# A six-layer decoder on one core: convolution by taps, one projection, and diagonal matrices in a state-space scan

## The chip, the cores and the metric

One core of one Trainium2 chip runs the whole program. The metric is the device time of one execution in microseconds (us); a profiled execution also gives a span, from the first to the last instruction.

## The reference, cut to what matters

Eight sequences of 128 tokens of width 128 (fp32) go through six residual stages, each followed by a layer norm. Stages 1, 2 and 5 are attentions with 16 heads of width 8 (the second and third over a context of 77 tokens), stage 3 is a small mixture, stage 6 a mixture of 8 experts. The change is mostly in stage 4:

```python
scores = gelu(xn @ r_w1 + r_b1) @ r_w2 + r_b2       # one score a token
topk 32 tokens of 128 -> small attention; the other 96 tokens, in order -> state space
xi, z  = split(x_ssm @ in_w)                        # 2 x 256 channels
xc     = silu(conv_b + sum_j shift_j(xi) * conv_w[:, j])         # 4 taps
dtp, Bm, Cm = xc @ xproj_w                          # 8 + 16 + 16 columns
delta  = softplus(dtp @ dt_w + dt_b)
h_t    = exp(delta * A) * h_(t-1) + (delta * xc) * Bm            # 16 states a channel
y      = (sum_s h * Cm + xc * Dp) * silu(z)
x + scattered(y @ out_w, attention output)
```

## The kernel before

Each engine has one instruction stream written by hand, in its own block; the streams meet only at semaphores, and each runs strictly in the order in which it is written. PSUM has 8 banks of 512 fp32 columns. Two rings (`aring`, banks 0 to 3, emptied by ScalarE; `dring`, banks 4 to 7, emptied by VectorE) hand products over in the order of two job lists. `keep_busy` issues idle bf16 products where TensorE would otherwise stand still.

**Stage 4 ahead of the scan** (span 157 to 227 us). VectorE normalises the tokens (XH, L1112), TensorE transposes them and forms the router's scores; VectorE ranks all 128 scores against each other (L1124 to L1132, with a product with `before` on GpSimd in the middle, L568), a product with `after` counts positions (L1582), and L1140 makes a permutation matrix `Perm` for each sequence. TensorE applies it (L1589) to give `xpT`, channels by tokens with the 96 state-space tokens ahead of the 32 chosen ones. The convolution is four accumulated products for each half of the channels and of the tokens, with `conv_w` multiplied into the input weights beforehand (`convin`, L556, L1611). The small attention has its queries masked for each group (`qGa`, L574), 32 score products (L1623), a softmax on VectorE (L1150 to L1160) and 32 output products (L1657), all ahead of the scan. `delta` comes out of xc through a folded weight `Wdt` (L1635), B out of products that use xc as weights (L1641), C out of products of their own (L1648) and goes by DRAM to all partitions. ScalarE and VectorE form the softplus (L763 to L769, L1171 to L1188). Four products give z (L1662). `du` = delta * xc is turned by 12 TensorE transposes (L1704).

**The scan** has 32 steps n (16 states times two halves h of the channels, state s = n // 2). For each state ScalarE scales `duT` by the column of B (`scale`, L795, six pieces of 128x256) and makes two decays (L783). For each step TensorE runs `inputs(n)`, six transposes into one of two PSUM buffers (L1682), VectorE the scan instruction (L1198), GpSimd the product with C (L589), and TensorE `accumulate(n-3)`, 768 columns added through the identity into banks 0 to 2 (L1695). `xD` = xc * Dp (GpSimd, L579) starts those banks.

**After the scan** the gated y and the small attention's output go through their output weights (L1723, L1732) and back to their places through `PermT` (L1741), whose transposes are made ahead of the convolution (L1606).

**The attentions** (`attention_tensor`, `attention_scalar`, `attention_vector`) share a pipeline over the 8 sequences. The weighted values of every sequence go to bank 6 (`weigh`, L1377), so `weigh(7)` waits for `normed`, that is until VectorE has read sequence 6 out of that bank. In the endings, `between` puts other work (transposes of the first half of the result) after iteration B = 8.

The lines that carry most of the argument:

```python
def inputs(n):                                   # TensorE, L1675
    for k in range(NK):                          # NK = 6
        ins = nc.tensor.transpose(dBu[n % NDB][:, 128 * k:128 * (k + 1)],
                                  scaled[s % 2][k][:, 128 * h:128 * (h + 1)], ident[:])
```

Of the kernel before, what the change touches and what calls it, by code (L numbers as in the profile page):

```python
# [28 lines left out]
H, HD = 16, 8  # L29
# [11 lines left out]
NH = DIN // 128  # L41
E1, IW = 8, 256
# [62 lines left out]
class Attention:  # L105


    def __init__(self, sem, name, nk, scale, kM, V, Wo, XB, Xout, masked=False):
# [12 lines left out]
        self.recip_ready = sem(f"{name}_recip_ready")  # L121
# [3 lines left out]
        self.stats_ready = sem(f"{name}_stats_ready")  # L125
        self.var_ready = sem(f"{name}_var_ready")
# [17 lines left out]
    def wait_bank(self, pe, what, i, g=0):  # L144

        if what == "flip" and i >= B:
            pe.wait_ge(self.exp_ready, G * B)
            self.wait_flip_read(pe, i - 1)
            return
        place = PLACE[what, i, g] - len(RING_BANKS)  # L150
        if place >= 0:
# [10 lines left out]
            + ["xnT.0", "xnT.1", "router.0", "router.1", "srow.0", "srow.1", "W5T", "xprojT", "Wdt.0", "Wdt.1", "k5.0", "k5.1", "v5.0", "v5.1", "xpT.0", "xpT.1"]  # L162
            + ["qa", "ka", "permT.0", "permT.1"] + [f"conv.{h}.{c}" for h in range(2) for c in range(2)]
            + [f"delta.{h}.{c}" for h in range(2) for c in range(2)] + [f"z.{h}.{c}" for h in range(2) for c in range(2)]
            + ["x4T.0", "x4T.1", "q5.0", "q5.1", "x5T.0"])
DVE_JOBS = (["kv.0", "kv.1", "kv.2", "kv.3", "v1.0", "k1.1", "v1.1", "q2.0", "q2.1"]
            + ["pooled", "logits8", "cexp", "cT", "up.0", "up.1", "scol"]
            + ["cumU", "va", "BT", "C.0", "C.1", "dposA.0", "dposA.1", "dposS.0", "dposS.1", "dl.0", "dl.1", "x5T.1", "logits6"])
# [8 lines left out]
def _build(nc, ctx, a, out):  # L177
# [11 lines left out]
    before = sb("before", [128, 128])  # L189
# [3 lines left out]
    groupmask = sb("groupmask", [128, G])  # L193
# [30 lines left out]
    Wqkvo4 = sb("Wqkvo4", [128, 4, D]); bqk4 = sb("bqk4", [128, 2]); bv4 = sb("bv4", [128, D])  # L224
    posbias = sb("posbias", [128, D])
    inw4 = sb("inw4", [128, 2 * DIN]); convw = sb("convw", [128, DIN, DC]); convb = sb("convb", [128, NH])
    convin = sb("convin", [128, DC, DIN])
    xprojT = sb("xprojT", [DTR, NH, 128])
    Wdt = sb("Wdt", [128, NH, DIN])
    xproj = sb("xproj", [128, NH, DTR + 2 * DS]); dtw = sb("dtw", [DTR, DIN]); dtb = sb("dtb", [128, NH])  # L230
# [67 lines left out]
    def row(ap, p=128):  # L298
# [26 lines left out]
               (bv4[:], row(a["L1_attn_bv"]))]  # L325
# [3 lines left out]
                (convw[:], a["L1_attn_conv_w"].rearrange("(o n) c -> o n c", o=1).to_broadcast([128, DIN, DC])),  # L329
                (convb[:], a["L1_attn_conv_b"].rearrange("(h p) -> p h", p=128)),  # L330
                (xproj[:], a["L1_attn_xproj_w"].rearrange("(h p) n -> p h n", p=128)),
                (dtw[:], a["L1_attn_dt_w"]), (dtb[:], a["L1_attn_dt_b"].rearrange("(h p) -> p h", p=128)),
# [24 lines left out]
    def spare(t):  # L357
# [3 lines left out]
    dA = [big[:, (2 + i) * W768:(3 + i) * W768] for i in range(2)] + [spare(X[0])]  # L361
# [6 lines left out]
    scaled = [[att[:, 1536 + 256 * k:1536 + 256 * (k + 1)] for k in range(NK)],  # L368
              [qTflat[:, 256 * k:256 * (k + 1)] for k in range(4)] + [att[:, 3072 + 256 * k:3072 + 256 * (k + 1)] for k in range(2)]]
    hst = [big[:, (6 + i) * W768:(7 + i) * W768] for i in range(2)] + [spare(sq)]  # L370
    hC = [big[:, (8 + i) * W768:(9 + i) * W768] for i in range(2)] + [spare(XB), spare(ctxN)]
    NDA, NDB, NHS, NHC = len(dA), len(dBu), len(hst), len(hC)
    kM2flat = kM2[:].rearrange("p j b n -> p (j b n)")
    xD = kM2flat[:, 0:2 * W768]
# [3 lines left out]
    sp_abs = big[:, 2 * W768:4 * W768].rearrange("p (h n) -> p h n", h=NH)  # L378
    sp_exp = big[:, 4 * W768:6 * W768].rearrange("p (h n) -> p h n", h=NH)
    sp_log = big[:, 6 * W768:8 * W768].rearrange("p (h n) -> p h n", h=NH)  # L380
    sp_relu = big[:, 8 * W768:10 * W768].rearrange("p (h n) -> p h n", h=NH)
    PADT = DC - 1 + T
    xpT = sb("xpT", [128, B, PADT])
    hrT = big[0:D // 2, 2 * B * T:3 * B * T].rearrange("p (b t) -> p b t", b=B)
    Srow = big[:, 0:B * T].rearrange("p (b t) -> p b t", b=B)
    scol = sb("scol", [128, B]); gt = big[:, B * T:2 * B * T].rearrange("p (b t) -> p b t", b=B); eq = V2full[:, 2 * NH * W768:2 * NH * W768 + B * T].rearrange("p (b t) -> p b t", b=B)
    rank = sb("rank", [128, B]); ties = sb("ties", [128, B]); sel = sb("sel", [128, B]); unsel = sb("unsel", [128, B]); cumU = sb("cumU", [128, B])
    pos = sb("pos", [128, B]); posa = sb("posa", [128, B])
    Perm = gt; PermT = eq
    qTa = ctxT[:].rearrange("p b t -> p (b t)")[:, 0:B * KSEL].rearrange("p (b k) -> p b k", b=B); kMa = att[:, 1536:1536 + J * B * KSEL].rearrange("p (j b k) -> p j b k", j=J, b=B); va = R[:, 0:2, :]  # L390
    Pa = convw[:].rearrange("p n c -> p (n c)").rearrange("p (n k) -> p n k", k=KSEL)
    PaT = XB[:].rearrange("p b d -> p (b d)").rearrange("p (n k) -> p n k", k=KSEL)
    mxa = sb("mxa", [128, 2 * H]); sma = sb("sma", [128, 2 * H])
    oaT = R[:, 4:6, :]
    oa_heads = Pa
    qGa = att[:, 3072:4096].rearrange("p (g b k) -> p g b k", g=G, b=B)
    Crows = att[0:DS, 0:W768]
# [19 lines left out]
    def _(sp):  # L417
# [4 lines left out]
        dring.wait_copied(sp, "C.1")  # L422
# [20 lines left out]
    def _(pool):  # L443
# [13 lines left out]

        P_.memset(ones_col[:], 1.0)
# [6 lines left out]
        P_.memset(before[:], 0.0)  # L465
# [89 lines left out]
        for j in range(DC):  # L555
            ins = P_.tensor_tensor(out=convin[:, j, :], in0=inw4[:, 0:DIN], in1=convw[:, :, j], op=ALU.mult)  # L556
# [40 lines left out]
    def _(act):  # L597
# [124 lines left out]
        for c in range(2):  # L722
            copy_out(f"srow.{c}", half(Srow, c), bank4, bias=rb2[:])
# [1105 lines left out]
```

## Time and profile before

| | us |
|---|---|
| median of 3 runs | 460.2 (457.71 to 460.31) |
| the profiled execution | 459.13 |
| its span | 457.3 |
| mean granted TensorE clock | 0.976 of full speed |

The profile is of one execution. A line number is that of the kernel before. In the chain of waits each piece is what the next one waited for; a fp32 product has two records (x2) for each matmul, a transpose one. Matmul records overlap, so the pitch (time of a run of them in the chain, divided by their count) is the price, not the length of one record.

### The profile page before, as it was taken

The numbers are of one execution on the slowest core, as the hardware profiler recorded it, in microseconds if no ns is written. First come the engines' busy times: TensorE is split into PE (matmuls) and PEld (weight loads), VectorE is DVE, ScalarE is ACT, GpSimd is POOL, SyncE is SP. The second block draws the span as 40 slices with busy tenths as digits, with TensorE's granted clock in tenths as the row PEclk, the third lists the DMA queues.
The fourth block names the chain that finished last, engine by engine and source line by source line (L and its number), as shares of the span: only waits on it lengthen the run. The fifth ranks groups of instructions, "written<-read, shape, count | busy, mean of one in ns | idle before, by whom it ended". The sixth has DMA issues, their size and how long they took to land.

```text
span 457.3 us, 9931 instructions
## 1 busy us (share of the span) xinstructions
PE 404.7 (88%) x3990; PEld 265.1 (58%) x3990; DVE 284.4 (62%) x697; ACT 234.2 (51%) x433; POOL 138.6 (30%) x118
## 2 busy tenths in 40 slices
PE   3788998999989978997689999989999799999992
PEld 2445675546765836662466666754677456666662
DVE  5785985754757554326499888763466554444546
ACT  1225654737567055766699999314455552222220
POOL 5829643300013124130098989310001100000001
PEclk9899999999999988998899999999999999999997
DMA  7320000000000000003013332052000000000001
GB/s 184 78 72 1 3 4 2 1 3 1 4 4 0 1 0 2 1 0 93 16 69 97 112 97 76 1 187 90 3 3 4 2 0 1 0 0 2 0 1 46
DMA packets 17023, 14.42 MB, mean 32 GB/s; under 512 B 6435, under 2 KB 14147, under 8 KB 16979
## 3 DMA queue, kind: packets, MB, share of 16 engines
q1 hardware_dynamic: 15680, 13.09, 9.7%
q10 hardware_dynamic: 1299, 0.71, 0.5%
q8 instruction: 32, 0.52, 0.5%
q14 instruction: 12, 0.10, 0.1%
HBM read 13.22 MB, written 0.57 MB: 30 GB/s over the span
## 4 chain that ended last, share of the span: by engine, by line
PE 69%; DVE 13%; ACT 11%; issue 3%; DMA 1%; POOL 1%; ACTq 0%; POOLq 0%; DVEq 0%
PE PS L1695 7%; PE PS L1756 6%; PE PS L1760 6%; PE PS L1369 6%; PE PS L1787 6%; PE PS L1315 4%; PE PS L1301 4%; PE PS L1348 4%; ACT att L633 3%; PE PS L1682 3%; PE PS L1384 3%; PE PS L1611 2%; ACT att L795 2%; PE PS L1431 2%; PE PS L1310 2%
## 5 line engine op out<-in xcount | busy, mean ns | idle before, releaser
L633 ACT ACTIVATE att<-PS 77x512 f32<-77x512 f32 (+1 forms) x96 | 51.7, 591 | 45.7 <-PE PS L1372 45.7
L904 DVE TENSOR_REDUCE mxp<-PS 128x4 f32<-128x308 f32 (+1 forms) x96 | 48.0, 537 | 31.8 <-PE PS L1348 31.8
L496 POOL TENSOR_TENSOR rstd<-ve,neg_half 128x1 f32<-128x1 f32 x24 | 13.3, 556 | 120.1 <-DVE ve L966 120.1
L830 ACT ACTIVATE kM<-PS 128x512 f32<-128x512 f32 x32 | 19.1, 597 | 56.3 <-PE PS L1756 56.3
L1198 DVE TENSOR_TENSOR_SCAN big<-big,PS 128x768 f32<-128x768 f32 x22 | 38.2, 1746 | 7.2 <-PE PS L1682 7.2
L1254 DVE TENSOR_TENSOR big<-kM,PS 128x512 f32<-128x512 f32 x32 | 21.9, 688 | 27.3 <-PE PS L1760 26.0
L490 POOL TENSOR_TENSOR rstd<-ve,neg_half 128x4 f32<-128x4 f32 x6 | 6.2, 1032 | 103.7 <-DVE ve L860 103.7
L1301 PE MATMUL PS<-negsel,identb 128*128 128x512 bf16 x140 | 33.9, 386 | 2.2 <-DVE big L1006 1.7
L1756 PE MATMUL PS<-xT,V 128*128 128x512 f32 x64 | 32.9, 596 | 0.8 <-DVE xT L1242 0.8
L1760 PE MATMUL PS<-xT,V 128*128 128x512 f32 x64 | 32.7, 592 | 0.0
L1787 PEld LDWEIGHTS PS<-big 128*128 128x128 f32 x256 | 29.7, 192 | 3.3 <-issue 3.3
L1787 PE MATMUL PS<-big 128*128 128x128 f32 x256 | 29.7, 275 | 0.0
L795 ACT ACTIVATE att<-big,BT 128x256 f32<-128x256 f32 x64 | 27.1, 492 | 0.7 <-DVE big L1202 0.7
L527 POOL TENSOR_TENSOR hr<-hvar,half_bh 77x8 f32<-77x8 f32 (+1 forms) x7 | 22.8, 3265 | 9.4 <-DVE hvar L887 9.4
L1301 PEld LDWEIGHTS PS<-negsel,identb 128*128 128x128 bf16 x140 | 13.1, 99 | 20.1 <-issue 4.5
L1372 PE MATMUL PS<-flipped,negsel 32*77 32x128 bf16 (+1 forms) x384 | 24.5, 216 | 0.0
L1695 PE MATMUL PS<-big,ident 128*128 128x512 f32 (+1 forms) x64 | 23.1, 486 | 0.0
L1275 DVE SCALAR_TENSOR_TENSOR R<-PS,aff,R 128x128 f32<-128x128 f32 x56 | 15.8, 345 | 11.2 <-PE PS L1787 11.2
L1369 PE MATMUL PS<-qT,kM 32*77 32x128 f32 x512 | 20.9, 276 | 1.8 <-ACT att L633 1.1
L783 ACT ACTIVATE big<-big,Aneg 128x760 f32<-128x760 f32 x22 | 19.6, 914 | 2.9 <-DVE big L1188 2.9
L1760 PEld LDWEIGHTS PS<-xT,V 128*128 128x128 f32 x64 | 12.2, 190 | 15.3 <-issue 14.8
L1682 PE MATMUL PS<-ident,att 128*128 128x128 f32 x128 | 19.4, 275 | 1.0 <-ACT att L795 1.0
(349 smaller groups left out, 896.7 us busy)
## 6 DMA issues: line engine op xcount, KB each, us to landing
kM<-Cdram SPq DMA_DIRECT2D x6, 384.0 KB, 3.5
XH<-Cdram SPq DMA_DIRECT2D x5, 384.0 KB, 3.4
xT<-Cdram SPq DMA_DIRECT2D x5, 384.0 KB, 3.4
V<-in_L_ffn_Wg SPq DMA_DIRECT2D x1, 1024.0 KB, 5.4
V<-in_L_ffn_Wu SPq DMA_DIRECT2D x1, 1024.0 KB, 8.0
convw<-in_L_attn_conv_w SPq DMA_DIRECT2D x1, 512.0 KB
out_x<-X SPq DMA_DIRECT2D x2, 256.0 KB, 2.3
ctxN<-in_ctx ACTq DMA_DIRECT2D x1, 308.0 KB
```

Of the source, the lines that this page charges most:

```text
L633: A_(PT[0:nk, i % 2, g], bank4(at.bank("exp", i, g), nk), ACT.Exp, scale=at.scale)\
L795: ins = A_(scaled[s % 2][k], duT[:, k, :], ACT.Identity, scale=BT[:, k, s:s + 1])
L904: V_.tensor_reduce(mxp[:, b % 3, g, 0:J], PS[:, at.bank("max", b, g), 0:J * nk].rearrange("p (j k) -> p j k", j=J), axis=AX.X, op=ALU.max) ...
L1198: V_.tensor_tensor_scan(hst[m % NHS], dA[m % NDA], dBu[m % NDB], 0.0, ALU.mult, ALU.add)\
L1301: M_(PS[:, bank, :], identb[:], negsel[:].rearrange("p j t -> p (j t)"), start=True, stop=True)
L1369: M_(PS[0:nk, at.bank("exp", b, g), j * T:(j + 1) * T], at.kM[rows(g), j, b, :], qT[rows(g), b, :], start=not at.masked, stop=False)
L1372: ins = M_(PS[0:nk, at.bank("exp", b, g), j * T:(j + 1) * T], negsel[rows(g), j, 0:nk], upper(flipped)[rows(g), (b - 1) % 2, 0:T], start=F ...
L1682: ins = nc.tensor.transpose(dBu[n % NDB][:, 128 * k:128 * (k + 1)], scaled[s % 2][k][:, 128 * h:128 * (h + 1)], ident[:])
L1695: ins = M_(y_piece(h, lo, hi), ident[:], hC[n % NHC][:, lo:hi], start=False, stop=(n // NH == DS - 1 and (h, lo) != (0, 512)))
L1756: M_(PS[:, n % 2, :], Wg6[:, e, i * 128:(i + 1) * 128], half(xT, c), start=True, stop=True)\
L1760: M_(PS[:, 2 + n % 2, :], Wu6[:, e, i * 128:(i + 1) * 128], half(xT, c), start=True, stop=True)\
L1787: ins = M_(PS[:, 4 + (2 * e + c) % 4, b4 * D:(b4 + 1) * D], hidE[e % 2][:, i, b * T:(b + 1) * T], Wd6[:, NI * e + i, :], start=(i == 0), s ...
```

## The change

1. **Convolution.** `token_in(b)`, eight products of 512 columns ahead of the permutation, gives xi and z of every token in token order (`XI`); `inner_inputs` then permutes xi (16 products of 96 columns). The first tap is a ScalarE activation, the other three taps are 12 multiply-adds on VectorE. `convin` and its products go.
2. **One projection.** `proj(c)` gives dt, B and C in 40 rows with two products a half; `delta_in(c)` uses 41 rows of it, one of them ones, so that the bias comes along. B is transposed out of it (6 small transposes). The softplus loses its Relu on ScalarE and works on halves of the tokens in place of halves of the channels.
3. **Ranking.** The sums over scores become 16 bf16 products with a column of ones; GpSimd is out of the chain.
4. **Small attention.** Values are made in four masked versions (32 products); the scores are taken by 32-row groups without `qGa`; weights are transposed on TensorE; 32 products of 32 columns and 4 of 256 (`weighted_values`) stand within the scan, after inputs(4), with the division by the sums on VectorE between scan instructions.
5. **z** is permuted within the scan: 16 products of 96 columns (`z_in`, after inputs 17, 19, 21, 23), with copies on ScalarE. `PermT` is made after the scan.
6. **Diagonals.** In place of scaling duT (128x256) and transposing, ScalarE makes six diagonal 128x128 matrices of B a state, and TensorE multiplies duT by them. `xc * Dp` becomes a product with a diagonal.
7. **Attention endings.** The last sequence's weighted values go to bank 4, `between` moves one iteration later, the flips of iterations 8 and 9 use banks 7 and 5 and wait for less. K and V of stage 5 are made before the router, partly on VectorE.

```diff
     def bank(self, what, i, g=0):
         if what == "flip" and i >= B:
-            return 7
+            return 5 if i == B + 1 else 7
...
+    def out_bank(self, b):
+        return 4 if b == B - 1 else 6
...
             def weigh(b):
-                if b:
+                if b == B - 1:
+                    at.wait_flip_read(pe, B - 2)
+                elif b:
                     pe.wait_ge(at.normed, b)
...
+        V_.tensor_tensor(lower, Srow, wide(scol[:], [128, B, T]), ALU.is_lt)
+        for b in range(B):
+            V_.scalar_tensor_tensor(equal[:, b, :], Srow[:, b, :], scol[:, b:b + 1], after[:], ALU.is_equal, ALU.mult)\
+                .then_inc(event("compared"), 1)
...
+        def token_in(b):
+            product(aring, f"XI.{b}", xT[:, b, :], inw4[:])
...
+        def inner_inputs(c):
+            pe.wait_ge(event("perm"), c + 1)
+            aring.wait_copied(pe, f"XI.{HB * c + HB - 1}")
+            for h in range(NH):
+                for b4 in range(HB):
+                    ins = M_(PS[:, 4 + NH * c + h, b4 * TS:(b4 + 1) * TS], XI[:, c * HB + b4, 0, 128 * h:128 * h + 128],
+                             Perm[:, c * HB + b4, 0:TS], start=True, stop=True)
...
+                    V_.scalar_tensor_tensor(a_, x_, convw[:, h, j:j + 1], a_, ALU.mult, ALU.add).then_inc(event("conv"), 1)
...
         def inputs(n):
-            pe.wait_ge(event("scaled"), s + 1)
+            if s:
+                pe.wait_ge(event("scaled"), s)
             if n >= NDB:
                 pe.wait_ge(event("h_ready"), n - NDB + 1)
             for k in range(NK):
-                ins = nc.tensor.transpose(dBu[n % NDB][:, 128 * k:128 * (k + 1)],
-                                          scaled[s % 2][k][:, 128 * h:128 * (h + 1)], ident[:])
+                ins = M_(dBu[n % NDB][:, 128 * k:128 * (k + 1)], duT[:, k, 128 * h:128 * (h + 1)], diagB[s % 2][:, k, :],
+                         start=True, stop=True)
...
         for n in range(1, NH * DS):
             inputs(n)
+            if n == 4:
+                weighted_values()
+            if n >= 17 and n % 2 and n < 25:
+                z_in((n - 17) // 2)
             if n >= 3:
                 accumulate(n - 3)
...
         def scale(s):
             for k in range(NK):
-                ins = A_(scaled[s % 2][k], duT[:, k, :], ACT.Identity, scale=BT[:, k, s:s + 1])
+                ins = A_(diagB[s % 2][:, k, :], ident[:], ACT.Identity, scale=BT[:, k, s:s + 1])
```

## Rows read from the trace of the kernel before

**Rows 1.** The page: its span.

```profile
span 457.3 us, 9931 instructions
```

**Rows 2.** The chain of waits before the scan: start us, us, engine, tile, line.

```profile
162.90 1.28 ACT L606
...
177.84 1.24 DVE big L1140
...
179.12 2.06 PE PS L1589 x16
...
189.41 7.95 PE PS L1611 x24
...
198.02 5.43 PE PS L1635 x16
203.44 2.58 PE PS L1641 x24
206.03 4.39 PE PS L1648 x8
```

**Rows 3.** Timeline of choosing the tokens: start, us, engine, line, operation, shapes.

```profile
168.44 0.17 DVE L1122 COPY scol<-PS 128x8 f32<-128x8 f32 x1 [4.60 <-PE PS L1562]
...
169.94 3.27 POOL L568 TENSOR_TENSOR V<-V,before 128x1024 f32<-128x1024 f32 x1 [8.16 <-DVE V L1124]
...
173.15 2.65 POOL L477 MEMSET V<- 77x3072 f32 x1
...
174.77 1.06 DVE L1131 TENSOR_SCALAR unsel<-rank 128x8 f32<-128x8 f32 x1
```

**Rows 4.** Groups by shape, 166 to 224 us: count, busy us, mean ns.

```profile
L1172 DVE TENSOR_TENSOR big<-big 128x768 f32<-128x768 f32 x2 | 1.9, 959 | 0.1
...
L1152 DVE TENSOR_TENSOR convw<-PS,mxa 128x256 f32<-128x256 f32 x4 | 1.4, 417 | 0.0
```

**Rows 5.** Chain of waits: other products with known shapes.

```profile
71.42 1.12 PE PS L1384 x32
...
379.11 3.57 PE PS L1787 x32
```

**Rows 6.** Windows: us, busy of PE, PEld, DVE, ACT, POOL, granted clock.

```profile
215.00:220.00 5.00, 0.00 (x0) 0.00 (x0) 4.86 (x10) 1.42 (x2) 0.00 (x0) 0.99 0.50 182
220.00:223.00 3.00, 2.79 (x13) 2.82 (x14) 0.94 (x2) 1.24 (x2) 0.00 (x0) 0.50 0.02 5
247.00:290.00 43.00, 42.83 (x214) 28.65 (x214) 38.48 (x23) 42.91 (x82) 39.64 (x22) 1.00 0.27 83
```

**Rows 7.** Timeline of the scan's first inputs and last sums.

```profile
226.76 1.50 PE L1682 MATMUL PS<-ident,att 128*128 128x128 f32 x12 [0.97 <-ACT att L795]
...
292.09 1.45 PE L1695 MATMUL PS<-ctxN,ident 128*128 128x256 f32 x4
```

**Rows 8.** The chain of waits within the scan.

```profile
230.65 2.40 ACT att L795 x6
233.05 0.82 ACT big L783
...
249.69 0.66 PE PS L1682 x6
250.34 1.29 PE PS L1695 x4
```

**Rows 9.** Groups by shape within the scan.

```profile
L1198 DVE TENSOR_TENSOR_SCAN big<-big,PS 128x768 f32<-128x768 f32 x22 | 38.2, 1746 | 7.2 <-PE PS L1682 7.2
...
L589 POOL TENSOR_TENSOR big<-big,kM 128x768 f32<-128x768 f32 x6 | 10.9, 1826 | 27.5 <-DVE big L1198 27.4
```

**Rows 10.** Timeline at the ends of the first and third attention.

```profile
70.11 1.08 ACT L633 ACTIVATE att<-PS 128x512 f32<-128x512 f32 x2
...
355.16 1.07 ACT L633 ACTIVATE att<-PS 77x512 f32<-77x512 f32 x2
...
361.73 1.06 PE L1756 MATMUL PS<-xT,V 128*128 128x512 f32 x2
```

More of the change, by code:

```diff
@@ L390, in _build @@
[L390 to L393, printed above, removed]
+    Perm = X[0]; PermT = masks.rearrange("p (b t) -> p b t", b=B)
@@ new lines, in _ @@
+        negated_exp(0)
+        act.wait_ge(event("small_attention"), 1)
+        A_(Pa[:], Pa[:], ACT.Exp, scale=1 / math.sqrt(HD)).then_inc(event("sp_exp"), 1)
+        negated_exp(1)
+        for c in range(2):
+            w = slice(c * W384, (c + 1) * W384)
+            act.wait_ge(event("sp_exp"), 2 * c + 1)
+            A_(sp_log[:, :, w], sp_exp[:, :, w], ACT.Ln, bias=1.0).then_inc(event("sp_log"), 1)
+        for k in range(2):
+            act.wait_ge(event("turned"), k + 2)
+            A_(half(PaT, 1 - k), bank4(1 - k), ACT.Copy).then_inc(event("chosen_copied"), 1)
@@ L812, in _ @@
                 decay(NH * s + 4)
-        A_(zs[:], zs[:], ACT.Silu).then_inc(event("z_ready"), 1)
+            if s == 0:
+                values_copy(1)
+            if 8 <= s < 12:
+                z_copy(s - 8)
+        act.wait_ge(event("z_copied"), 2 * NH)
+        A_(zs[:], zs[:], ACT.Silu).then_inc(event("z_gate"), 1)
+        for c in range(2):
+            act.wait_ge(event("turned"), c + 4)
+            A_(half(PermT, c), bank4(3 + 4 * c), ACT.Copy).then_inc(event("z_copied"), 1)
         for c in range(2):
@@ L1189, in _ @@
-        for h in range(NH):
-            dve.wait_ge(event("delta_ready"), h + 1)
-            V_.tensor_tensor(du[:, h, :], delta[:, h, :], xc[:, h, :], ALU.mult).then_inc(event("du_ready"), 1)
         def scan(m):
@@ L1548, in _, with values @@
             ins.then_inc(dring.full, 1)
-        loaded(pe, "l4")
-        x_transposed("xnT", XH, event("xh4"), 1, idle=15)
+        loaded(pe, "l5")
+        transposes("W5T", [W5[:, k, :] for k in range(4)], 128, 128)
+        aring.wait_copied(pe, "W5T")
+        product(aring, "k5.0", W5T[:, 1, :], half(ctxT, 0), cols=HB * NC)
+        def values(c):
+            row_products(dring, f"v5.{c}", [ctxT[:, b, :] for b in range(c * HB, (c + 1) * HB)], W5T[:, 2, :], NC)
+        values(0)
+        product(dring, "k5.1", W5T[:, 1, :], half(ctxT, 1), cols=HB * NC)
+        loaded(pe, "l4", "ssm")
+        x_transposed("xnT", XH, event("xh4"), 1, idle=2)
         for c in range(2):
@@ L1563, in _ @@
         ins.then_inc(dring.full, 1)
-        loaded(pe, "l5")
-        transposes("W5T", [W5[:, k, :] for k in range(4)], 128, 128)
-        loaded(pe, "ssm")
-        i = fill(aring, "xprojT")
-        for h in range(NH):
-            ins = nc.tensor.transpose(PS[0:DTR, i, h * 128:(h + 1) * 128], xproj[:, h, 0:DTR], ident[:])
-        ins.then_inc(aring.full, 1)
-        aring.wait_copied(pe, "xprojT")
-        for h in range(NH):
-            product(aring, f"Wdt.{h}", xprojT[:, h, :], dtw[:], cols=DIN)
@@ L1576, in _ @@
-        aring.wait_copied(pe, "W5T")
-        for c in range(2):
-            product(aring, f"k5.{c}", W5T[:, 1, :], half(ctxT, c), cols=HB * NC)
+        for b in range(1, 5):
+            token_in(b)
+        i = fill(dring, "rank")
+        for b in range(B):
+            pe.wait_ge(event("compared"), b + 1)
+            M_(PS[:, i, b:b + 1], lower[:, b, :], onesb[:], start=True, stop=False)
+            ins = M_(PS[:, i, b:b + 1], equal[:, b, :], onesb[:], start=False, stop=True)
+        ins.then_inc(dring.full, 1)
```

619 lines of the change are left out of this document (338 added, 281 removed).

## The prediction, made before the change was run

> **What bounds the kernel now.** I read the chain of waits first, because it tells where time can be won at all, then the windows for busy time and clock, then groups by shape for prices. The span is 457.3 us [rows 1]. The change touches four stretches of it.
>
> Ahead of the scan the chain is a relay: TensorE's products, one engine's reading of them, the next products [rows 2]. Its long pieces are the convolution (7.95), the folded delta product (5.43), B (2.58) and C (4.39). Nothing there overlaps well: from 215 to 220 us TensorE does nothing while VectorE ends the softplus, and its granted clock is 0.50, 1.2 GHz, in the next 3 us [rows 6]. The first transposes of the scan start at 226.76 and its last sum ends at 292.09 + 1.45 = 293.54: the scan is 66.8 us [rows 7].
>
> Within the scan three engines are nearly level. A state costs ScalarE 2.40 + 2 x 0.82 = 4.04 us. It costs TensorE two steps of 0.66 (six transposes) and 1.29 (768 columns of sums), 3.90 [rows 8]. VectorE needs 2 x 1.75 = 3.49 and GpSimd 2 x 1.83 = 3.65 [rows 9]. From 247 to 290 us ScalarE is busy 42.91 of 43.00 us and TensorE 42.83, at full clock [rows 6]. So ScalarE leads by only 0.14 us a state: whatever is taken off it is worth little unless TensorE gets cheaper too.
>
> **The change: the scan.** A fp32 product with 128x128 weights and 128 columns costs 3.57 / 16 = 0.223 us (x32 are two records for each of 16 products) [rows 5]. A fp32 transpose of the same size costs 0.66 / 6 = 0.11 [rows 8]. inputs(n) replaces six of these by six of those: 1.34 in place of 0.66. A step is then 1.34 + 1.29 = 2.63 us of TensorE against 2.02 now, +0.61, and 32 steps give **+19.5**. ScalarE gets cheaper: 256 columns take 0.40 and 760 take 0.82 [rows 8], so 0.83 ns a column and 0.29 for 128; a state is 6 x 0.29 + 1.64 = 3.4 us. It is hidden now, as are VectorE and GpSimd. The gain on ScalarE goes nowhere, and TensorE is the only bound, with no slack.
>
> That changes the cost of what is moved into the scan, all of it on TensorE. weighted_values: 32 products with 32-column weights. The nearest row has 16 of them, of 128 columns and in four column groups, in 1.12 us, 0.07 each [rows 5], so 2.0 at most for the 32 with shorter columns, and 0.4 for the four sums of 256 columns: 2.4. Bounds: 1.0 (half the columns' price) and 3.9 (the four sums without overlap, 3 x 0.43 more). z_in: 16 products of 96 columns with 128x128 weights. L1641 is such a case with 16 columns, 2.58 / 12 = 0.215 each [rows 2], so it is the weights that bound them: 16 x 0.22 = 3.5. The four z products of now lie under VectorE's softplus and free nothing. The diagonal of Dp replaces products through the identity of the same columns: nothing on TensorE. From first inputs to last sum: 32 x 2.63 = 84.2, the third start product 0.86 (512 of 768 columns of 1.29), 0.4 of waiting for the first scans, 2.4 and 3.5: 91.4, against 66.8. **Scan: +24.6** (22 to 27).
>
> Here the Trainium skill (TensorE: Matmul & The Clock Gate, Part 4: PE-mode transpose) speaks otherwise: it gives about 275 ns for a 128x128 transpose in a kernel's context. By that the six would cost 1.65 us and the change would save 0.3 us a step. The trace disagrees: the record of one is that long, but the pitch is 0.11 us, so that figure is a latency here and not a price.
>
> **Ahead of the scan.** All on the clock of the profile.
> - *Router.* W5T, k5.0, v5.0 and k5.1 now stand before the first turned token. They are about 3.5 us and the wait that hides them is as long, less 0.5. v5.1 and token_in(0) come between router and scores, +1.0, partly in gaps. The table load of 1.28 in the chain goes [rows 2]. Net -0.4.
> - *Ranking.* Now from the scores' column at 168.44 to the permutation at 177.84 it is 9.4 us [rows 2, 3], with GpSimd's 3.27 in the middle and a 1.06 us comparison of 8 columns that ends together with GpSimd's memset [rows 3]. After: the column 0.2, one comparison 1.2 (the size of L1140), eight of 128 columns at 0.25 (0.2 to 0.35), sums by TensorE and two thresholds 0.5, counting and positions 1.0: 4.95. -4.4. But token_in 5 to 7 (3 x 0.86) stand before `inner_inputs` in TensorE's order, so it starts at about 174.8 and not at 173.6.
> - *To xc.* From 174.8: three groups of eight products with full weights, 1.8 each, q and k 0.9, 32 value products 2.2 at 0.07 [rows 5]: TensorE is free at 183.3. VectorE has 12 multiply-adds of up to 384 columns. 768 columns take 0.96 [rows 4], 1.25 ns a column; reading PSUM, 256 take 0.36 (1.42 / 4), 1.4 ns: 0.5 each (0.45 to 0.7), 6.2 in all, ending at 183.3, the second half held by inner_inputs(1). Then two Silus behind four key copies: xc is whole at 185.5. Now it is at 189.41 + 7.95 + 0.6 = 198.0 [rows 2]. With the two items above, -12.5.
> - *To the first inputs.* Now 198.0 to 226.76, 28.8 us. After: projection, small scores (32 in 16 tiles, 1.1 to 2), delta_in for the first half, the same for the second (1.28 a pair of 384-column products), and VectorE's copy of the second half behind two small-attention operations of 1.2: 5.0 us, 190.5. Abs, Exp (0.84 each for 768 columns), a table load (1.28), two Ln (0.8 each) on ScalarE: 4.7, 195.2 [rows 2, 8]. Four operations of 0.96 [rows 4] in series on VectorE, of which the first starts before the second Ln ends: 198.6. The transposes at 1.2 GHz, since TensorE will have idled about 4.6 us as it did before 220 [rows 6], y_start in its way, and the copy of duT: 201.9. B's 24 products, C's 8 and the folded delta products are gone. 16.4 us, so -12.4.
>
> Sum: first inputs at 201.9 and not 226.76, **-24.9** (-27.5 to -21.5: low prices for comparisons, taps and small scores; or taps at 0.7 and the chain's unseen waits).
>
> **After the scan.** PermT's eight transposes, 8 x 0.11, now stand before the attention's output product: **+0.9** (0 to 1.3).
>
> **Endings.** weigh(7) starts at 71.42 [rows 5], after normed; its last exponentials end at 70.11 + 1.08 = 71.19 [rows 10], and three of its four groups could go earlier. So about 1.0 earlier in attention 1; TensorE then also does not queue transposes ahead of the last flips, nor ScalarE two copies: 1.7. Attention 2: 1.0 and little more, as the hidden products are issued by TensorE without a gap: 1.2. Attention 3: 355.16 + 1.07 against products of the first expert at 361.73 [rows 10], with a longer normalisation to skip: 1.7. **-4.6** (-5.5 to -2.8). The layer norm of the last sequence is next in line each time and moves with it.
>
> Sum: +24.6 - 24.9 + 0.9 - 4.6 = -4.0. From the profile's own 459.13 that is 455.1; the median of the runs is 1.1 above that execution, so **456.2**.
>
> **Rivals.**
> 1. *The products cost more than their best row.* L1589 is eight fp32 products of 128x128 by 128 in 2.06 us [rows 2], 0.258 each, with a ring wait in them. If all products by fresh full weights run so, the 192 of the scan cost 6.7 more and the 40 of z and of the permutations 1.4: 464.3; with the taps at 0.7, 466. It decides from 0.240 a product on (4.0 / 232 above 0.223): beyond that the kernel is slower than before. For it: the weights change at every product. Against it: they do in L1787 too.
> 2. *The relay shortens by more.* Small products hide in column groups and in waits, the waits between VectorE's small steps vanish: low ends of the prologue and of weighted_values, 456.2 - 2.6 - 1.4 - 0.9 (endings) = 451.3.
> 3. *The scan does not become TensorE's.* If a product cost no more than a transpose, the step would be GpSimd's 1.83, the scan some 23 us shorter than I say, 433. All rows of fp32 products speak against it. The Trainium skill's figure for a transpose would make this direction stronger still: at 0.3 saved a step in place of 0.61 added, some 29 us below the forecast, 427; the pitch of 0.11 excludes it.
>
> **Chances.** The forecast, 453.5 to 460: 0.50. Rival 2, 449 to 453.5: 0.22. Rival 1, 460 to 466: 0.20. Rival 3: 0.02. Beyond 466: 0.06. A measurement of this kernel can tell about 1% (4.6 us). Below 455.6 lie rivals 2 and 3 and a third of the forecast: 0.40. Above 464.8 lie the last case and 0.3 of rival 1: 0.12. The range 450 to 463 leaves out about 0.2.
>
> **What would show it.** In the profile after: L1682's successor at 0.22 us a product and a step of 2.6 us; TensorE without gaps from the first sum on, ScalarE with gaps; first inputs near 202 and a last sum near 293, so that the gain ahead of the scan is spent within it; the last `weigh` 1 us after its predecessor's transposes, not 1.5. Wrong if the step is 2.0 (rival 3) or over 2.75 (rival 1), if the first inputs are before 199 or after 206, or if the endings keep their length.

## The result, and the profile after

The changed kernel takes 460.83 us (median of 19 runs, 459.02 to 464.32), the kernel before 459.57 (19 runs, 456.36 to 460.31): ratio **1.0045**, 95% interval 1.0026 to 1.0065. By the ratio it is 2.1 us slower (the medians alone are 1.3 apart), where I forecast 4.0 less. The profiled execution is the slowest of its 19, 464.32 us with a span of 462.5, so I also read a second one of the same kernel (`after_again` below, 462.08 us with a span of 460.3).

I cut the span at points that both kernels have: the first and last layer-norm output of each attention (L956 before, L994 after, eight each), the copy of the scores' column (L1122, L1169), the permutation matrix (L1140, L1186) and the first and last sum of the scan (L1695, L1793). Each number is the distance of two starts on the timeline:

| stretch | before | after | after_again | forecast of the difference |
|---|---|---|---|---|
| attention 1, first to last sequence | 19.60 | 18.84 | 18.85 | -1.7 |
| to attention 2's first sequence | 41.14 | 41.18 | 41.17 | 0 |
| attention 2, first to last | 18.92 | 18.18 | 18.17 | -1.2 |
| to the scores' column | 29.11 | **32.16** | **32.29** | -0.4 |
| ranking, to the permutation matrix | 9.40 | 5.38 | 5.39 | -4.4 |
| to the first sum of the scan | 54.04 | 37.44 | 36.48 | -20.1 } +4.5 |
| first to last sum | 60.21 | 82.41 | 82.41 | +24.6 } |
| last sum to the layer norm behind it | 10.75 | 11.62 | 11.62 | +0.9 |
| to attention 3's first sequence | 41.23 | **42.94** | 41.23 | 0 |
| attention 3, first to last | 20.77 | 20.42 | 20.39 | -1.7 |
| to the end | 92.46 | 92.48 | 92.51 | 0 |

The two rows with a brace belong together (my forecast parted them at the first inputs, the table parts them at the first sum). In the second profile their differences are -17.56 and +22.20, so +4.6. The two large terms came out close to the forecast; the sign was lost in the rows in bold and in the endings.

VectorE's timeline of the changed kernel while the tokens are chosen answers to [rows 3]: start, length, engine, line, operation, shapes. Eight comparisons of 128 columns take 2.18 us, and GpSimd's product is gone.

```profile
170.01 1.23 DVE L1171 TENSOR_TENSOR V<-big,scol 128x1024 bf16<-128x1024 f32 x1
171.15 2.18 DVE L1173 SCALAR_TENSOR_TENSOR V<-big,scol,after 128x128 bf16<-128x128 f32 x8
...
175.19 1.29 DVE L1186 TENSOR_TENSOR X<-colnum,pos 128x512 f32<-128x512 f32 x2
```

The chain of waits from there to the scan answers to [rows 2]:

```profile
177.10 1.76 PE PS L1667 x16
178.86 1.73 PE PS L1675 x16
180.59 1.84 PE PS L1667 x16
182.43 0.89 PE PS L1681 x4
183.32 1.89 PE PS L1686 x64
...
199.33 1.54 PE PS L1803 x6
200.87 1.71 PE PS L1764 x2
202.57 1.28 PE PS L1803 x6
```

The convolution's 7.95, the folded delta's 5.43 and the 2.58 and 4.39 of B and C are gone. The transposes of du (L1803) cost 1.54 for six where a step of the scan before had 0.66 [rows 8]: TensorE's granted clock is 0.5 there.

The chain within the scan answers to [rows 7, 8]. L1780 is inputs, L1793 the sums, L1753 z:

```profile
205.75 1.34 PE PS L1780 x12
...
248.31 1.29 PE PS L1793 x4
249.60 1.34 PE PS L1780 x12
250.94 0.87 PE PS L1753 x8
251.81 1.32 PE PS L1793 x4
...
291.33 5.16 PE PS L1793 x16
```

Apart from one scan instruction of VectorE at its start (1.76 us at 209.32), nothing but TensorE stands in it: a step is 1.34 + 1.29 = 2.63 us, and six products are 1.34, 0.223 each. The 32 small products of the small attention are 0.66 (L1738) and its four sums 0.47 (L1741); z is 0.87 four times. From the first inputs to the end of the last sum it is 205.75 to 296.49, 90.7 us; I forecast 91.4.

What I had not priced stands at the end of attention 2. The timeline of the changed kernel, VectorE, GpSimd and TensorE:

```profile
137.55 2.66 POOL L481 MEMSET V<- 77x3072 f32 x1
137.65 2.63 DVE L994 TENSOR_SCALAR X<-R,mv,rstd 128x128 f32<-128x128 f32 x1 [0.66 <-POOL rstd L500]
...
140.43 0.48 PE L1564 MATMUL PS<-ones_col,X 128*128 128x1 f32 x2 [1.61 <-DVE X L994]
```

and of the kernel before at the same place:

```profile
139.26 0.86 POOL L556 TENSOR_TENSOR convin<-inw,convw 128x256 f32<-128x256 f32 x1
139.33 0.87 DVE L956 TENSOR_SCALAR X<-R,mv,rstd 128x128 f32<-128x128 f32 x1 [0.66 <-POOL rstd L496]
```

The other 23 instances of this VectorE operation take 0.34 to 0.35 us. Here it starts 0.1 us behind a GpSimd instruction and ends with it, in both kernels; but the change put the clearing of attention 3's value tile (`value_ones(V5)`, out of GpSimd's part in the ranking) behind attention 2, and that one is 2.66 us long. TensorE waits 1.61 us for it, and in this execution its clock falls behind the wait. The windows of the changed kernel (us, then busy time of PE, PEld, DVE, ACT and POOL; granted clock, DMA share, GB/s):

```profile
138.00:146.00 8.00, 6.39 (x33) 3.61 (x31) 4.68 (x15) 4.85 (x8) 4.83 (x5) 0.79 0.00 0
196.00:206.00 10.00, 6.45 (x22) 5.09 (x24) 6.88 (x11) 9.68 (x18) 0.00 (x0) 0.66 0.22 84
306.00:316.00 10.00, 7.94 (x30) 3.37 (x28) 4.18 (x19) 2.39 (x4) 2.08 (x2) 0.83 1.03 310
```

Three dips to 1.2 GHz. The first is new, the second answers to the one at 220 [rows 6], the third comes in some executions only. One dip is gone: while it ranked the scores, from 170 to 176 us, the kernel before was granted 0.54, and the changed one has 1.00 there.

### The profile page after: what moved, and what is told of

Its sections match the earlier page's. It is cut to its first block, busy times and chain, and to the rows that moved or that the text cites. A ratio compares the mean times of both kernels' runs of the same rounds, so it can differ in the third digit from the quotient of the medians.

```text
span 462.5 us, 10452 instructions
## 1 busy us (share of the span) xinstructions
PE 416.9 (90%) x4240; PEld 288.9 (62%) x4251; DVE 288.6 (62%) x713; ACT 223.7 (48%) x428; POOL 131.4 (28%) x122
## 4 chain that ended last, share of the span: by engine, by line
PE 76%; DVE 12%; ACT 6%; issue 4%; DMA 1%; POOL 1%; ACTq 0%; POOLq 0%; DVEq 0%
PE PS L1780 9%; PE PS L1793 9%; PE PS L1869 6%; PE PS L1873 6%; PE PS L1432 6%; PE PS L1900 6%; PE PS L1378 5%; ACT att L637 3%; PE PS L1411 3%; PE PS L1449 3%; PE PS L1364 3%; PE PS L1496 2%; ACT outT L648 2%; PE PS L1611 2%; DVE XH L905 2%
## 5 line engine op out<-in xcount | busy, mean ns | idle before, releaser
L1793 PE MATMUL PS<-att,ident 128*128 128x512 f32 (+1 forms) x96 | 34.8, 488 | 0.0
L593 POOL TENSOR_TENSOR att<-big,kM 128x768 f32<-128x768 f32 x9 | 16.4, 1818 | 50.7 <-DVE big L1257 49.9
L1364 PE MATMUL PS<-negsel,identb 128*128 128x512 bf16 x108 | 26.4, 381 | 3.6 <-DVE big L1040 1.8
L1780 PEld LDWEIGHTS PS<-att,big 128*128 128x128 f32 x192 | 24.0, 192 | 4.3 <-issue 3.8
L1780 PEld LDWEIGHTS PS<-qT,big 128*128 128x128 f32 x192 | 23.8, 192 | 4.5 <-issue 4.1
L1780 PE MATMUL PS<-qT,big 128*128 128x128 f32 x192 | 24.1, 275 | 0.6 <-DVE big L1257 0.6
L1780 PE MATMUL PS<-att,big 128*128 128x128 f32 x192 | 24.0, 275 | 0.0
L1257 DVE TENSOR_TENSOR_SCAN untransposed<-untransposed,PS 128x768 f32<-128x768 f32 x10 | 17.5, 1752 | 9.3 <-PE PS L1780 9.2
```

What stands on the lines that cost most here:

```text
L1257: V_.tensor_tensor_scan(hst[m % NHS], dA[m % NDA], dBu[m % NDB], 0.0, ALU.mult, ALU.add)\
L1364: M_(PS[:, bank, :], identb[:], negsel[:].rearrange("p j t -> p (j t)"), start=True, stop=True)
L1780: ins = M_(dBu[n % NDB][:, 128 * k:128 * (k + 1)], duT[:, k, 128 * h:128 * (h + 1)], diagB[s % 2][:, k, :], start=True, stop=True)
L1793: ins = M_(y_piece(h, lo, hi), ident[:], hC[n % NHC][:, lo:hi], start=False, stop=(n // NH == DS - 1 and (h, lo) != (0, 512)))
```

## The experiments

Twelve kernels in three groups of four; each group shares a chip and its 17 runs of the kernel before (457.92, 459.10 and 458.15 us), so ratios are compared, not times (a difference of two ratios is given in us of a kernel of 458 or 459 us). My theory at the start had two parts: A, the fp32 products bind the scan and spend what the stretch ahead of it wins; M, a memset at the end of attention 2 and the clock behind it account for the miss.

### The diagonals taken back (after_turned_scan)

```diff
             for k in range(NK):
-                ins = A_(diagB[s % 2][:, k, :], ident[:], ACT.Identity, scale=BT[:, k, s:s + 1])
+                if s == 0 and k == NK // 2:
+                    act.wait_ge(event("first_inputs"), 1)
+                ins = A_(scaled[s % 2][k], duT[:, k, :], ACT.Identity, scale=BT[:, k, s:s + 1])
...
-                ins = M_(dBu[n % NDB][:, 128 * k:128 * (k + 1)], duT[:, k, 128 * h:128 * (h + 1)], diagB[s % 2][:, k, :],
+                ins = nc.tensor.transpose(dBu[n % NDB][:, 128 * k:128 * (k + 1)],
+                                          scaled[s % 2][k][:, 128 * h:128 * (h + 1)], ident[:])
```

> The changed kernel, with the diagonals of B alone taken back: ScalarE scales duT again (128x256, six pieces a state, the first three as soon as its own copy of duT is there) and TensorE turns the pieces with six transposes a step. Everything else of the change stays, the small attention's products and z within the scan too. Theory A (the scan is bound by TensorE, and six fp32 products at 0.223 us in place of six transposes at 0.11 took back what the stretch ahead of it won): TensorE's step falls from 2.63 to 1.95 and ScalarE leads with 4.04 us a state; the scan is 16 x 4.04 + about 3 for the copies of z on ScalarE + 1 of start = 69 in place of 90.7, the first inputs come 1 to 2 us later since scale(0) is in front of them: 440 to 443 us, ratio about 0.96. Rival B (it is the work moved into the scan, 36 small products and 16 of z, that costs it, not the diagonals): the scan stays at 85 or more, ratio 0.99 to 1.00.

444.75 us, ratio 0.9695 (0.967 to 0.9719). Theory A holds, rival B falls: first to last sum is 66.64 us in place of 82.41. The chain:

```profile
240.37 1.60 ACT qT L828 x4
241.96 0.40 ACT att L828
242.36 0.40 ACT scaledx L828
242.76 1.64 ACT big L818 x2
...
260.07 0.66 PE PS L1782 x6
260.73 1.29 PE PS L1795 x4
```

Up to 248 us ScalarE sets the pace with 2.40 + 1.64 a state, as before the change; from z's second group of products on TensorE does, 0.66 + 1.29 = 1.95 a step. The gain is 16.1 us and not the 18 to 21 I expected. The scan, from the first inputs to the end of the last sum, takes 73.4 us and not 69: I had ScalarE pace it to the end, with 3 us for its copies of z, but from 248 us on TensorE does, and z's products stand in the chain with 1.13 and twice 0.87. How the 4.4 divides was not taken apart. Ahead of it, three of ScalarE's pieces (1.30) now stand in the chain.

### The diagonals alone (before_diagonals)

```diff
-                ins = A_(scaled[s % 2][k], duT[:, k, :], ACT.Identity, scale=BT[:, k, s:s + 1])
+                ins = A_(scaled[s % 2][k][:, 0:128], ident[:], ACT.Identity, scale=BT[:, k, s:s + 1])
...
-                ins = nc.tensor.transpose(dBu[n % NDB][:, 128 * k:128 * (k + 1)],
-                                          scaled[s % 2][k][:, 128 * h:128 * (h + 1)], ident[:])
+                ins = M_(dBu[n % NDB][:, 128 * k:128 * (k + 1)], duT[:, k, 128 * h:128 * (h + 1)],
+                         scaled[s % 2][k][:, 0:128], start=True, stop=True)
```

> The kernel before, with the diagonals of B alone: ScalarE makes six 128x128 diagonals a state, TensorE multiplies duT by them; nothing else of the change. Theory A: a step of TensorE goes from 2.02 (set by ScalarE) to 2.63, 32 x 0.61 = +19.5, less 0.7 for the shorter scale(0) ahead of the first inputs: 478 to 480 us, ratio 1.041. Rival B: no more than +5, 465. Rival C (a product costs no more than a transpose and the scan becomes GpSimd's): faster than before.

476.57 us, ratio 1.0403 (1.0375 to 1.0432), +18.5 us. Its chain in the scan, from the first sum to the last, has the same two prices and nothing else:

```profile
250.69 1.34 PE PS L1682 x12
252.02 1.29 PE PS L1695 x4
```

First to last sum is 77.51 against 60.21, and from the first inputs to the end of the last sum it is 85.5 against 66.8, 18.8 more. The changed kernel's first to last sum, 82.41, is 4.9 above 77.51: z and the small attention, which I had at 5.9.

### The memset spread (after_ones_spread)

```diff
-        attention_pool(at2)
-        value_ones(V5[:])
         step(P_.memset(colmask[:], 0.0))
...
+        def value_ones5():
+            if (part := next(parts, None)) is None:
+                return
+            if part < B // 2:
+                ins = P_.memset(V5[:, 2 * part:2 * part + 2, :, HD:VW], 0.0)
...
+        attention_pool(at2, value_ones5)
```

`colmask`'s memset, an unchanged line, stands ahead of attention 2 by this and no longer behind it.

> The changed kernel, with GpSimd's clearing of the value tile of attention 3 (one memset of 77x3072, 2.66 us, right behind its last work for attention 2) cut into four of 77x768 that stand behind its small powers for sequences 0 to 3, and the mask's memset ahead of attention 2. Theory M (VectorE's normalisation of sequence 7, 2.63 us under the memset where the same takes 0.87 elsewhere, is held by it, and TensorE's idling behind it lowers its clock): 1.8 off at the operation and up to 1 for the clock, 457 to 458.5 us, ratio to the kernel before 0.995 to 0.999. Rival N (that profile's long operation is of that execution, or the wait is covered): no change against the changed kernel, ratio 1.0045.

460.61 us, ratio 1.0048 (1.0029 to 1.0066): no gain in time, the number of rival N. But the profile shows the mechanism of theory M:

```profile
138.32 1.16 POOL L454 TENSOR_SCALAR_AFFINE_SELECT colmask<-colmask 128x512 f32<-128x512 f32 x1
138.41 1.15 DVE L1004 TENSOR_SCALAR X<-R,mv,rstd 128x128 f32<-128x128 f32 x1 [0.67 <-POOL rstd L500]
```

VectorE's operation now lasts as long as the mask's select, 1.15 us, the granted clock from 138 to 146 us is 1.00, and the way to the scores' column is 29.64 us, 2.65 less than in after_again. What became of it, by the same stretches against after_again: 0.46 on the way to attention 2, 0.46 on the way to the first sum of the scan and 1.47 between the scan and attention 3 are given back, and attention 3 is 0.70 shorter. The 1.47 is where the windows show the granted clock at 0.83:

```profile
138.00:146.00 8.00, 7.42 (x44) 4.13 (x43) 4.92 (x19) 6.14 (x10) 2.21 (x3) 1.00 0.00 0
196.00:206.00 10.00, 8.43 (x38) 6.34 (x39) 6.30 (x10) 7.92 (x15) 0.00 (x0) 0.69 0.03 12
306.00:316.00 10.00, 8.36 (x37) 4.21 (x38) 3.38 (x12) 2.39 (x4) 1.01 (x1) 0.83 0.84 257
```

The first 0.46 is this edit's own, and the change's fault over again. The mask's memset was moved too, and at its new place it follows a GpSimd product that a VectorE operation is already held by (1.01 us in after_again, where the product ends at 86.0, against 0.22 for its other instance, of 77 rows); that operation now ends with the memset:

```profile
85.94 0.53 POOL L555 MEMSET colmask<- 128x512 f32 x1
85.08 1.47 DVE L935 TENSOR_SCALAR hvar<-hss 128x128 f32<-128x128 f32 x1
```

The way to attention 2 is 41.62 or 41.63 us in all seven profiles with the spread memset and 41.16 or 41.17 in those that have the change's memset, so the edit is worth 2.65 - 0.46 = 2.2 us in its stretches.

Over its 12 runs the mean granted clock is 0.979, over the 19 of the changed kernel 0.982, on another chip. That the kernel with the spread memset has other dips more often fits this; that the edit causes them, no run shows.

### The old endings (after_old_endings)

```diff
-            return 5 if i == B + 1 else 7
+            return 7
...
-        return 4 if b == B - 1 else 6
+        return 6
...
-                if b == B - 1:
-                    at.wait_flip_read(pe, B - 2)
-                elif b:
+                if b:
...
-        attention_tensor(at1, {B + 1: x1_half, B + 2: mixture_weights}, 0)
+        attention_tensor(at1, {B: x1_half, B + 1: mixture_weights}, 0)
```

> The changed kernel, with the endings of all three attentions as in the kernel before: the weighted values of the last sequence in bank 6 and waiting for normed, the other work one iteration earlier, the flips of iterations 8 to 10 in bank 7 one behind the other. The pooled sums stand in bank 5. The memset of the value tile stays where the change put it. My prediction priced the endings at -4.6, so taking them back would cost 4.6: 465.4, ratio 1.0145. Theory E (the traces: attention 1 gives 0.98, attention 3 some 0.35, attention 2 nothing that the memset leaves): +1 to +2.5, ratio 1.007 to 1.010. Rival F (what comes next in line is late anyway): 0.

464.56 us, ratio 1.0137 (1.0109 to 1.0164), 3.6 to 4.2 us more than the changed kernel's two measurements: in time this is nearer to my 4.6 than to theory E. In its profile the three attentions take 19.58, 18.91 and 20.70 us from first to last sequence, against 18.85, 18.17 and, without the 0.7 us of issue that after_again has there, 19.7: 0.73, 0.74 and 1.0, in all 2.5. It has the dip behind the scan (0.83), which costs some 1.6 us and is no part of the endings. The memset still holds the last sequence for 2.63 us and TensorE waits 1.74 us, but the clock does not fall behind it (1.00 from 138 to 146 us). That splits the loss ahead of the router: its stretch is 31.12 us here and 29.64 with the same endings and the memset spread (below), so the stall alone is 1.5; the dip adds 1.0 to 1.2 in the two profiles of the table. Why the clock falls behind one such wait and not behind the other, no run shows.

### The changed kernel again (after_again)

> The changed kernel itself once more, on the same chip as the next three, so that differences of 1 to 4 us between variants of it are read on one chip. Its first measurement was 1.0045 of the kernel before; 1.003 to 1.008 is expected. Its profile should again have the long normalisation of sequence 7 in attention 2 (2.6 us, under the memset) and, behind the scan, first products of attention 3 at half clock.

461.62 us, ratio 1.0058 (1.0038 to 1.0078). The long operation is there again, 2.63 us, and so is the dip behind it. The third dip is not:

```profile
138.00:146.00 8.00, 6.40 (x22) 3.21 (x20) 5.21 (x15) 5.24 (x8) 5.14 (x5) 0.79 0.00 0
196.00:206.00 10.00, 6.15 (x28) 4.55 (x29) 7.34 (x11) 9.75 (x18) 0.00 (x0) 0.66 0.24 89
306.00:316.00 10.00, 7.95 (x42) 3.49 (x41) 4.75 (x21) 2.39 (x4) 1.70 (x2) 1.00 0.99 306
```

Half of the expectation fell: the dip behind the scan is not a property of the kernel.

### Old endings, memset spread (after_old_endings_ones_spread)

Both edits above.

> The changed kernel with the old endings of the attentions and with the memset of the value tile spread. With after_again, after_ones_spread and after_old_endings it makes the four corners of endings and memset. In the profiles the endings are worth 0.75, 0.75 and 1.03 us in the three attentions, 2.5 in all, the times said 4.2 (1.0137 against 1.0045, on two chips). If 2.5 is right: ratio 1.0048 + 0.0055 = 1.010. If the memset's stall costs more with the old endings: lower than after_old_endings by 2 us or more, 1.009. If the endings are worth my predicted 4.6: 1.015.

461.51 us, ratio 1.0068 (1.0045 to 1.009), below what 2.5 us for the endings would give. The endings are worth 0.9 us in this pair (1.0068 against 1.0048, with intervals that overlap), the spread memset 3.2 (1.0137 against 1.0068), as the branch of the expectation has it in which the stall costs more with the old endings. In time each edit seems to give another amount with the other in place. The profiles do not bear that out: the first two attentions are 19.57 and 18.91 us, as in after_old_endings, and the way to the scores' column is 1.5 us shorter by the spread memset where it is 2.65 shorter with the new endings. What differs besides is where the clock dips, and the kernels that are compared here ran on two chips.

### More idle products ahead of attention 3 (after_idle20)

```diff
-        x_transposed("x4T", X[0], event("x4"), 1, idle=14)
+        x_transposed("x4T", X[0], event("x4"), 1, idle=20)
```

> The changed kernel with 20 idle bf16 products in place of 14 ahead of the first transposes of attention 3, so that TensorE has no gap of 1.4 us there. In the three profiles with diagonals in the scan TensorE's granted clock is 0.5 for some 3.4 us from there on, in the two with transposes it is not, and the way from the layer norm to the first output of attention 3 is 1.6 us longer. Theory G (it is the gap that the clock answers to): the dip goes, 1.6 us off, ratio 0.0035 below after_again. Rival H (the dip goes back to what TensorE did before the gap, or moves on to the next gap): no change.

460.43 us, ratio 1.0032 (1.0009 to 1.0055) beside 1.0058 (1.0038 to 1.0078): inconclusive, since the intervals overlap and the control beside it had no dip either. Theory G is not shown. Its profile has no dip behind the scan, but a longer one behind attention 2: the way to the scores' column is 33.86 us, 1.6 more than in after_again. Nor did the pattern hold from which I started, a dip behind the scan with diagonals and none with transposes: after_again has diagonals and no dip, the next kernel transposes and the dip (in its profile the way from the scan to attention 3 is 1.7 us longer than in after_again).

### Diagonals back, memset spread, idle products ahead of du's transposes (turned_scan_spread_busy)

The edits of after_turned_scan and after_ones_spread, and this:

```diff
+        pe.wait_ge(event("relu_added"), 1)
+        keep_busy(4, 20)
         for c in range(2):
             pe.wait_ge(event("du_ready"), c + 1)
```

> The changed kernel with the diagonals of B taken back as in after_turned_scan, the memset of the value tile spread, and 20 idle bf16 products in TensorE's wait ahead of the transposes of du, where its granted clock falls to 0.5 for 6 us in every profile. after_turned_scan is 0.9695; the spread memset gives 0 to 2.5 us, and at full clock the 12 transposes (1.54 + 1.49) and the starts of y (1.7 + 1.9) take 3.3 us less on TensorE, of which 1.5 to 2.5 are in the chain: 439 to 442, ratio 0.960 to 0.966. Rival: the clock falls later instead, 0.9695.

441.97 us, ratio 0.9635 (0.9613 to 0.9657). The transposes of du and the starts of y run at full clock, but the 20 products, of which the first were at half clock, took 6.13 us and were in the way:

```profile
189.66 1.52 PE L1742 MATMUL PS<-ident,Pa 128*128 128x128 f32 x8
190.97 6.13 PE L1377 MATMUL PS<-negsel,identb 128*128 128x512 bf16 x20
196.93 0.82 PE L1817 MATMUL PS<-ident,untransposed 128*128 128x128 f32 x6
```

### The same with the old endings (spread_busy_old_endings)

> turned_scan_spread_busy (0.9635) with the old endings of the three attentions. In the profiles the new endings are worth 0.75, 0.75 and 1.02 us from the first to the last layer norm of an attention; the times of two pairs said 4 and 0.9 us, with the clock's dips in other places. 2.5 us: ratio 0.969. My predicted 4.6: 0.9735.

444.38 us, ratio 0.9678 (0.9647 to 0.9709), 0.0043 or 2.0 us above the kernel with the new endings. The three pairs give 4.2 (or 3.6), 0.9 and 2.0 us, the profiles 2.5. The 0.9735 that my 4.6 asked for lies outside this interval; the first pair alone would not have excluded it.

### The same with diagonals (spread_busy_diagonals)

> turned_scan_spread_busy with the diagonals of B back in, so the changed kernel with the memset spread and 20 idle products ahead of the transposes of du. The scan from its first to its last sum is 82.4 us with diagonals and 66.6 with transposes, less about 1 for scale(0) ahead of the first sums: +15 to +16 on 441.97, 457 to 458, ratio 0.996 to 0.999. If the change fails by its scan alone, no repair outside of it makes it faster than the kernel before by 1%.

457.69 us, ratio 0.9986 (0.9966 to 1.0006). This is the changed kernel with its two repairs outside the scan: no longer slower than the kernel before, and not faster by 1% either. Against 0.9635 the diagonals cost 16.1 us, the same as in the first pair. Its transposes of du start right behind the idle products, with the clock up:

```profile
191.19 4.26 PE L1374 MATMUL PS<-negsel,identb 128*128 128x512 bf16 x19
195.63 0.87 PE L1815 MATMUL PS<-ident,untransposed 128*128 128x128 f32 x6 [0.17 <-DVE untransposed L1252]
```

### Without the idle products (turned_scan_spread)

> turned_scan_spread_busy without the 20 idle products: after_turned_scan with the memset spread alone. If the gain from 0.9695 to 0.9635 is the memset's (2.6 us between the last sequence of attention 2 and the router in the profile): 0.964 to 0.966. If it is the clock ahead of the scan: 0.968 to 0.970.

441.77 us, ratio 0.9654 (0.9623 to 0.9684). From 0.9695 the memset gives 1.9 us, close to the 2.2 of its stretches; the 20 idle products give 0.9 more. In both steps the intervals overlap, and this one reaches into the other branch of the expectation.

### Fourteen idle products, and twenty ahead of attention 3 (turned_scan_spread_busy14)

Against turned_scan_spread_busy:

```diff
-        keep_busy(4, 20)
+        keep_busy(4, 14)
...
-        x_transposed("x4T", X[0], event("x4"), 1, idle=14)
+        x_transposed("x4T", X[0], event("x4"), 1, idle=20)
```

> turned_scan_spread_busy with 14 idle products ahead of the transposes of du in place of 20 (the 20 took 6.13 us, and the transposes came 7.27 us behind those of the small attention in place of 5.93), and 20 in place of 14 ahead of attention 3. 1.3 us off ahead of the scan if the clock still rises with 14, up to 1.6 off where the dip behind the scan was: 0.957 to 0.962. If 14 leave the clock at 0.5: 0.9635 to 0.966.

**440.02 us, ratio 0.9603** (0.9579 to 0.9627): the lowest ratio of the study, 18.1 us below the kernel before on that chip; its interval overlaps with that of the 20 products (0.9613 to 0.9657), and which of its two edits gives what was not taken apart. All three places are at full clock in its profile:

```profile
138.00:146.00 8.00, 7.41 (x43) 4.11 (x42) 5.30 (x20) 5.92 (x9) 1.83 (x2) 1.00 0.00 0
190.00:200.00 10.00, 8.23 (x46) 4.74 (x47) 8.22 (x15) 8.82 (x14) 0.00 (x0) 1.00 0.36 123
286.00:296.00 10.00, 9.18 (x47) 4.12 (x47) 4.78 (x21) 2.39 (x4) 1.50 (x2) 1.00 0.97 301
```

## Why the prediction was wrong

It said 4.0 us less, it was 2.1 more; the time lies in the range that I gave, the direction is wrong. Point by point:

- *The scan, +24.6.* Right: +24.0 in the chain. The product's price of 0.223 and the step of 2.63 held to the last digit in two kernels, and both experiments on the diagonals found their cost: +18.5 alone against my 19.5, 16.1 when taken back. The first inputs start at 205.8 us, and at 205.0 in the second profile, for 201.9: later than forecast, within the bounds of 199 and 206. The weighted values were 1.1 in place of 2.4, z 3.5 as forecast. That TensorE alone binds it is shown: undoing the diagonals gives back nearly what they cost, and ScalarE takes the lead again. The groups of the page agree, VectorE's scans have waited 20.0 us for TensorE's inputs and ScalarE's decays 19.0 for the scans (busy, mean ns, idle before it and who ended it):

```profile
L1257 DVE TENSOR_TENSOR_SCAN big<-big,PS 128x768 f32<-128x768 f32 x22 | 38.6, 1754 | 20.7 <-PE PS L1780 20.0
...
L816 ACT ACTIVATE big<-big,Aneg 128x760 f32<-128x760 f32 x22 | 20.4, 930 | 19.0 <-DVE big L1257 19.0
```

- *Ahead of the scan.* Ranking -4.0 for -4.4. From the permutation on -18.4 in the chain for -20.1; in the second profile the whole up to the last sum is +4.6 for +4.5. (The 24 and 8 products of B and C that I named are records; they are 12 and 4 products. No term rests on it.)
- *After the scan, +0.9.* Right, 0.87.
- ***Endings, -4.6: mis-sized.*** The mechanism is right, weigh of the last sequence starts earlier in all three, but the last layer norm comes 0.75, 0.75 and 1.0 us sooner and not 1.7, 1.2 and 1.7: 2.5. In after_again weigh of the last sequence starts 0.74 us sooner behind the first layer norm than before, in attention 1 and in attention 2 alike, and not 1.0; the chain from there was as long as before, so the queueing that I had added on top (0.7 and 0.2) gave nothing. Taking the endings back cost 2.0, 0.9 and 4.2 us.
- ***Router, -0.4: the step that failed.*** I wrote that the products moved in front of it hide in a wait. Nearly all do: with the memset out of the way the stretch is 29.64 against 29.11, 0.9 off my figure. But I followed the engines' products and copies only, and let GpSimd's moved memset go without a price at its new place, though [rows 3] show it at 2.65 us and show a VectorE operation of 8 columns beside it that lasts 1.06 us. The Trainium skill (SBUF — State Buffer, Who interferes with whom) states that GpSimd shares a pair of ports with VectorE, that `tensor_scalar` can be among the operations that take it, and that the one that comes second is blocked for the whole instruction. The trace agrees, with 2.63 under 2.66 and 1.15 under 1.16. The stall (1.5) and the clock behind it (1.0 to 1.2) make the stretch 3.1 to 3.2 us longer than before in the table's two profiles; it is 2.0 longer in after_old_endings, where the clock does not fall, and 4.8 in after_idle20.

The balance of the table's second profile: its span is 3.0 us longer than before (460.3 against 457.3) and not 4.0 shorter, 7.0 off. The router is 3.6 of that, the endings 2.7 (2.1 in the sizes above, and 0.7 us of issue in attention 3 that not every execution has), the ranking 0.4, the way from the permutation to the last sum 0.1. In time the forecast is 6.1 off (4.0 + 2.1). The slowest execution has 1.7 more from a dip ahead of attention 3, which others do not have.

What is shown and what is not. That the memset holds VectorE is shown by two kernels and lengths that match, and by the mask's memset at its new place. That moving it is worth its 2.2 us in time is not: it gave 1.9 and 3.2 us in two pairs, of which the first is within the noise, and nothing in the third, where the profile shows dips of the clock elsewhere. What makes the clock fall in one execution and not in the next stays open. And no single experiment turned the changed kernel into a faster one by over 1% except taking the diagonals back.

*The rivals.* The first gave 464.3 and is nearest in time among those on the slow side, but for a reason that is out: the products are at 0.223 and not 0.258. The second fell but for its small products. The third is out. None of them was the one that happened: a stall outside of the scan, at a place where the change had only moved something. A forecast of -4 out of terms of +25 and -25 hangs on such things.

## What to carry to other kernels

If two of three engines in a loop are level, an edit that unloads one by loading the other costs its whole price in every pass: here 0.61 us in 32 steps, which used up most of a gain of 22 us that was real. Price every instruction that a change moves at its new place, on GpSimd too, and look at which VectorE operation starts just behind it; the repair of the memset repeated the mistake on a small scale. And where a change gains in one stage and loses in another, build the kernel that has only the gain: it was 3% faster than the kernel before (0.9695), and 4% with the two repairs outside the scan (0.9603).

## What the hardware showed that I had not expected

- VectorE's 128x128 normalisation (0.34 us alone) took 2.63 under a GpSimd memset of 2.66, 1.15 under a select of 1.16, and 0.87 under a GpSimd product of two inputs of 0.86. Another one (1.01 us under a GpSimd product) took 1.47 when a GpSimd memset of 0.53 followed the product.
- Runs of one kernel differ by their granted clock. The 12 of after_idle20 stand in steps: 0.988 at 458.3 to 458.6 us, 0.985 at 459.2 to 460.0, 0.981 at 460.9 to 461.3, 0.978 at 463.0 and 463.2. The steps are 1.2 to 2.1 us apart, as much as several terms of the sum; one dip behind the scan is 1.5 to 1.7 us of its stretch.
- With idle products ahead of them, the first six transposes of du took 0.82 to 0.88 us, without them 1.54. But idle products can be in the way: 20 of them took 6.13 us with the first at half clock, and 4.26 us (19 recorded) in another kernel at full clock.
